# A decoder of two layers: values issued in pairs of steps, key and query stacks loaded in two parts, and the second layer's projections half by half

## The chip, the cores and the metric

The kernel runs on 1 core of a Trainium2 chip. The time is that of the device, in microseconds (us), from one launch to its end; of several runs the median is given. Engines: TensorE (PE), VectorE (DVE), ScalarE (ACT), GpSimd (POOL), and SyncE (SP), whose queue issues all the DMAs.

## The reference, cut to what matters

Four batch elements (B = 4) of T = 1024 rows with D = 256 columns, and for each a context of S = 154 rows. Every sublayer is a residual with a layer norm (eps 1e-5) ahead of it:

```python
# layer 0: causal attention of 16 heads of 16, keys and values gated by a memory of Pluecker lines
scores = einsum('bhtd,bhsd->bhts', q, k_enh) * SCALE; softmax over s <= t; @ v_enh; @ out_w + out_b
# layer 0: cross attention to the context, rotary q and k, causal mask over s <= t
# layer 0: feed forward, rows and weights quantised, depthwise convolution of 3, silu
# layer 1: full attention, 16 heads of 16
q, k, v = jnp.split(x @ w_in.T + b_in, 3, axis=-1)
w = softmax(einsum('bhqd,bhkd->bhqk', q, k) / sqrt(d)); out = einsum('bhqk,bhkd->bhqd', w, v) @ w_out.T + b_out
# layer 1: one wide head over the context; then 16 experts of 128, the best 2 of each row, and a shared one
```

## The kernel before, in words

`build_program` (from L233) writes one program for each engine, and each runs through the same trip four times, one for each batch element (`tensor_program` at L2106, `scalar_program`, `vector_program`, `gpsimd_program`, `sync_program` at L2185). Nothing orders the engines but semaphores: `up(name, key)` marks an instruction, `at(name, key)` is the value to wait for. A trip has these stages: gated projections, heads of the first layer ("own"), output projection, cross attention ("cross"), feed forward ("feed"), heads of the second layer ("second"), the wide head, the experts.

**Stacks.** Scores are matmuls in bf16 of parts. A query or key value in f32 is cut into high, middle and low parts of bf16: ACT writes the high part, DVE the rest, ACT the middle part, DVE or POOL the low one. A head's stack has 96 rows, six parts of 16 rows (STACK = 6), so that one product sums the six part products. Queries and keys of all heads lie in `q_cut` and `k_cut` as slots [6, 2, 1024] (L505 to L520): queries high, middle, low, high, middle, high; keys high three times, middle twice, low. The repeated slots are copied: `double_queries` at L1169 and `double_keys` at L1174, each a copy of 2048 columns and one of 1024, on DVE or POOL. Then SP moves each head of a pair of heads with one DMA of 192 KB, 16 partitions x 6 slots into 96 rows (`load_queries` L860, `load_keys` L866). There are 3 places for pairs of the own and second heads and 6 for queries of the cross heads; the cross keys of all 16 heads are moved before, in 16 DMAs of 28.9 KB (`context_sync`, L1351).

**Order of the heads.** `attention_plan` (L160) writes one list of pieces, and each engine goes through it and does its own. `main` is the list of scores and values, a value step being put behind as soon as the scores of later steps make two groups; between entries of `main` come the pieces of the first pass, spread evenly. The pieces, with their lines:
- first (L646): scores of a tile of 128 rows with 512 keys into one of three banks (4 to 6), used in turn by first, top, spin, turn, context and wide pieces alike (`ring`, L591); DVE takes the maximum of each row (L796), which frees the bank.
- top (L725): the 32 maxima of a pair of heads, cut in three parts on POOL (L846 to L849), are transposed on PE, copied on ACT (L769), and a DMA of 12 KB (L909) puts them as three more rows of the query stack.
- score (L674; L678 the mask): both heads of a pair, 128 keys and up to 512 rows each, with those rows, into two banks; there are two such pairs of banks. ACT takes the exp of both in one instruction (L756), into one of four places in `probs`.
- value (L708): values of one step of 128 keys times the probabilities, two heads and odd and even tiles as four tiles of 32 columns of the array, summed up in bank 7. After the last step ACT copies it (gather, L763), PE transposes it (spin, L717) and DVE divides by the sum (norm, L812, L814).
- fill (L1438, `busy_tensor`): matmuls whose result nobody reads.

`heads_sync` (L877) is SP's order: first loads for all places, one after the other, then, in the order of the plan, top rows and the loads of the pair that takes a freed place.

**Around the heads.** `cross_vector`, `cross_scalar`, `cross_gpsimd` (L1370 to L1415) rotate and cut the cross queries in four units (half 0 of both groups of heads, then half 1), then double each group. In `tensor_program` 26 fillers and 6 more stand ahead of the cross heads. `feed_tensor` (L1440) ends with 26 fillers and the four turns (transposes, L481, copied by ACT, L488), 12 fillers between turns 1 and 2. `second_tensor` (L1571) then projects the keys and queries of the second layer in eight units of 4 matmuls: keys of group 0, half 0 and 1, queries of group 0, half 0 and 1, then group 1, and 9 fillers. `second_vector` and `second_gpsimd` cut and double them.

## Time and profile before

| | |
|---|---|
| median of 3 runs | 3350.33 us (3348.94 to 3357.76) |
| the profiled execution | 3356.7 us, its span 3355.1 us |
| mean granted TensorE clock | 0.996 |
| busy: PE, PEld, DVE, ACT, POOL | 95%, 51%, 69%, 53%, 19% |
| bytes by DMA | 147.74 MB, 18.1% of 16 engines' span on the hardware queue |
| trip 2 | 866 to 1694 us: own heads from 930, cross heads from 1113, feed from 1187, second heads from 1282 to 1495, experts to 1694 |

A matmul's end is modelled, and matmuls overlap by about 0.17 us, so a busy PE does not say that it is used to its limit: the starts do. Idle time in brackets stands before an instruction, with what ended it. A record of the value step comes twice for each matmul, since f32 goes through in two passes.

### The profile page before, as it was taken

Reading aid. Unit: us, or ns where it says so; the run is one execution under the profiler, and the core shown is the slowest. Engines: PE = TensorE matmul, PEld = TensorE weight load, DVE = VectorE, ACT = ScalarE, POOL = GpSimd, SP = SyncE. Lnnn points to the kernel's source line nnn. Section 1 sums busy time; section 2 is a strip of 40 time slices with the busy share of each in tenths; the row PEclk is TensorE's granted clock in tenths of the full one; section 3 lists DMA queues with packets and bytes.
Section 4 is the critical chain, followed back from the end, with each engine's and each line's share of the span. In section 5 each row is a group of like instructions: output and inputs, shape, how many; then the busy total and the mean of one; then the engine's idle time right before and its main releaser. Section 6 shows DMA issues by size and latency. Waiting matters only on the chain.

```text
span 3355.1 us, 46975 instructions
## 1 busy us (share of the span) xinstructions
PE 3191.1 (95%) x17720; PEld 1713.3 (51%) x17720; DVE 2323.0 (69%) x4331; ACT 1782.8 (53%) x2551; POOL 634.7 (19%) x1166
## 2 busy tenths in 40 slices
PE   6999889999999989999999998999999999899999
PEld 4444433378644443337864444334786444433477
DVE  7856688556685578856678557885667855788555
ACT  3565546643456555664355555566424655556632
POOL 0322010024132201012403120100340321020033
PEclk9999999999999999999999999999999999999999
DMA  3212011023121202111312020120231202021023
GB/s 138 51 34 39 1 34 34 11 65 114 32 52 26 40 1 38 30 35 53 115 38 43 18 40 1 39 39 25 63 105 42 40 17 39 5 44 30 10 84 96
DMA packets 118101, 147.74 MB, mean 44 GB/s; under 512 B 25384, under 2 KB 75920, under 8 KB 117596
## 3 DMA queue, kind: packets, MB, share of 16 engines
q1 hardware_dynamic: 117876, 144.74, 18.1%
q8 instruction: 141, 2.31, 0.3%
q14 instruction: 84, 0.69, 0.1%
HBM read 74.25 MB, written 4.46 MB: 23 GB/s over the span
## 4 chain that ended last, share of the span: by engine, by line
PE 51%; DVE 8%; ACT 4%; issue 2%; DMA 1%; SPq 1%; POOL 0%; DVEq 0%; ACTq 0%
PE psum L1908 13%; PE psum L708 9%; PE psum L674 8%; PE psum L646 7%; PE psum L1000 4%; DVE small L796 3%; ACT work L756 2%; PE psum L939 1%; PE psum L717 1%; PE psum L500 1%; DMA work<-work 1%; PE psum L481 1%; PE psum L929 1%; SPq L863 1%; PE psum L1734 1%
## 5 line engine op out<-in xcount | busy, mean ns | idle before, releaser
L796 DVE TENSOR_REDUCE small<-psum 128x1 f32<-128x512 f32 (+6 forms) x1856 | 1136.7, 656 | 210.2 <-PE psum L646 175.9
L756 ACT ACTIVATE work<-psum 128x1024 f32<-128x1024 f32 (+5 forms) x1024 | 918.3, 935 | 419.4 <-PE psum L674 317.4
L646 PE MATMUL psum<-work 96*128 96x512 bf16 (+4 forms) x2688 | 655.7, 308 | 32.8 <-DVE small L796 16.2
L1908 PE MATMUL psum<-rounded_work 128*128 128x512 f32 x2592 | 602.0, 394 | 9.9 <-DVE rounded_work L1994 6.5
L674 PE MATMUL psum<-work 99*128 99x512 bf16 (+4 forms) x2048 | 564.2, 358 | 6.9 <-ACT work L756 4.0
L1908 PEld LDWEIGHTS psum<-rounded_work 128*128 128x128 f32 x2592 | 489.9, 190 | 116.0 <-DVE rounded_work L1994 8.3
L708 PE MATMUL psum<-work 128*32 128x512 f32 (+4 forms) x4480 | 532.3, 528 | 1.6 <-ACT work L756 1.4
L646 PEld LDWEIGHTS psum<-work 96*128 96x128 bf16 x2688 | 233.5, 97 | 544.4 <-DVE small L796 332.2
L674 PEld LDWEIGHTS psum<-work 99*128 99x128 bf16 (+1 forms) x2048 | 178.5, 97 | 199.3 <-ACT work L756 63.1
L2009 ACT CAST rounded_work<-work 128x512 fp32r<-128x512 f32 x144 | 89.4, 621 | 344.5 <-DVE work L2050 321.7
L846 POOL CAST small<-small 128x16 bf16<-128x16 f32 x96 | 18.8, 196 | 1156.2 <-DVE small L803 586.8
L1438 PE MATMUL psum<-ident_bf 128*128 128x512 bf16 x808 | 201.3, 380 | 8.7 <-DVE work L1539 4.5
L812 DVE RECIPROCAL small<-psum 128x16 f32<-128x16 f32 x96 | 24.7, 257 | 243.1 <-PE psum L717 243.1
L2055 DVE TENSOR_TENSOR rounded_work<-work,rounded_work 128x512 fp32r<-128x512 f32 x144 | 118.4, 822 | 107.2 <-ACT rounded_work L2009 107.2
L1885 POOL CAST rounded_work<-work 128x256 fp32r<-128x256 f32 x192 | 100.3, 523 | 435.9 <-PE psum L1908 421.8
L708 PEld LDWEIGHTS psum<-work 128*32 128x32 f32 (+1 forms) x4480 | 94.0, 107 | 171.4 <-issue 143.9
L2045 DVE TENSOR_TENSOR work<-work,psum 128x512 f32<-128x512 f32 x144 | 98.7, 685 | 99.5 <-PE psum L1908 89.4
L1886 POOL TENSOR_TENSOR rounded_work<-work,rounded_work 128x256 fp32r<-128x256 f32 x192 | 148.1, 772 | 15.4
L1438 PEld LDWEIGHTS psum<-ident_bf 128*128 128x128 bf16 x808 | 77.8, 98 | 93.1 <-DVE work L1539 7.8
L2050 DVE TENSOR_TENSOR work<-work 128x512 f32<-128x512 f32 x128 | 114.2, 892 | 14.7 <-DMA work<-combine 10.4
L1000 PE MATMUL psum<-xT,qkv 128*128 128x512 f32 x256 | 113.1, 593 | 2.7 <-ACT xT L488 2.7
L1000 PE MATMUL psum<-xT,work 128*128 128x512 f32 x256 | 110.5, 592 | 0.0
(297 smaller groups left out, 3765.2 us busy)
## 6 DMA issues: line engine op xcount, KB each, us to landing
work<-work SPq DMA_DIRECT2D x320, 192.0 KB, 4.3
work<-combine SPq DMA_DIRECT2D x64, 512.0 KB, 4.1
work<-in_w_gate SPq DMA_DIRECT2D x64, 128.0 KB, 3.5
work<-in_w_up SPq DMA_DIRECT2D x64, 128.0 KB, 3.5
work<-in_w_down SPq DMA_DIRECT2D x64, 128.0 KB, 3.8
work<-in_x SPq DMA_DIRECT2D x8, 512.0 KB, 4.9
out<-x SPq DMA_DIRECT2D x8, 512.0 KB, 2.9
work<-work SPq DMA_DIRECT2D x64, 28.9 KB, 2.0
```

Of the source, the lines that this page charges most:

```text
L646: ins = nc.tensor.matmul(dst[:, c * n:(c + 1) * n], A.q_pair[0:ROWS, slot, h, P * i:P * (i + 1)], A.k_of(pair, h)[0:ROWS, s0:s0 + n], star ...
L674: ins = nc.tensor.matmul(dst[0:size, 0:P * many].rearrange("p (i c) -> p i c", c=P), A.k_of(pair, h)[0:MORE_ROWS, P * s:P * s + size], til ...
L708: ins = nc.tensor.matmul(dst, V_head, moving, start=(s == 0), stop=(s == A.ns - 1), skip_group_check=True)
L756: nc.scalar.activation(probs[0:size, n % 4, :, 0:P * many], banks(2 * (n % 2), 2)[0:size, :, 0:P * many], ACT.Exp, scale=DH ** -0.5).then_ ...
L796: nc.vector.tensor_reduce(tops[:, pair % 2, places[0]:places[-1] + 1:step], src, AX.X, ALU.max) \
L1000: ins = nc.tensor.matmul(out, w[:, a, P * k:P * (k + 1)], xT[:, a, 1 + HALF * half:1 + HALF * (half + 1)], start=(a == 0), stop=(a == KD - 1))
L1438: nc.tensor.matmul(bank(place).rearrange("p (a c) -> p a c", c=P), ident_bf[:, :], spread(ident_bf[:, :], 1, 4), start=True, stop=True, sk ...
L1885: pool_own(nc.gpsimd.tensor_copy(shape(hi_w), source))
L1886: ins = nc.gpsimd.tensor_tensor(shape(lo_w), source, shape(hi_w.bitcast(F32)), ALU.subtract)
L1908: ins = nc.tensor.matmul(dst, a_parts[i], b_parts[j], start=start and n == 0, stop=stop and n == 2, skip_group_check=True)
L2050: nc.vector.tensor_tensor(value, value, row[e % 2][:, HALF * half:HALF * (half + 1)], ALU.mult).then_inc(*up("unit_full", u))
L2055: nc.vector.tensor_tensor(hid_low[:, u % 4, :], value, hid_high[:, u % 4, :].bitcast(F32), ALU.subtract).then_inc(*up("unit_ready", u))
```

## The change

What it does:
- `attention_plan` puts two value steps of a pair behind one another, and `probs` has 6 places instead of 4.
- The slots are put in another order (queries middle, middle again, low, high; keys low, middle, high, high again): four slots instead of six are used, only one part is copied (512 or 1024 columns, `high_again`, `middle_again`, on POOL, for cross queries on ACT), and `double_queries` and `double_keys` are gone. A head's stack is moved in two DMAs: high parts of the queries (one slot read three times) and middle and low ones; of the keys middle to high again, and low to high. The first pair's upper half is moved before its low parts are cut.
- Cross keys are no longer moved ahead for all heads but by pair, with the queries, in the same way.
- The order of the second layer's units is keys and queries of half 0, then of half 1; unit 0 is projected between turns 1 and 2 of the feed stage.
- 12 fillers there become 2, 9 behind the units 2, 26 ahead of the cross heads 14. The second heads no longer wait for unit 6 at their entry, but their banks for units 4 to 6.
- wide_q is not kept for the whole run but loaded into freed space in each trip, after the last stacks.

```diff
+PROBS = 6
@@ attention_plan
-    def value(pair, s):
-        pieces = [("value", pair, s)]
-        if s == len(steps) - 1:
+    def values(pair, s):
+        pieces = [("value", pair, s), ("value", pair, s + 1)]
+        if s + 1 == len(steps) - 1:
...
-            while sum(len(steps[later]) for _, later in held[1:]) >= 2:
-                value(*held.pop(0))
-    for which in held:
-        value(*which)
+            while sum(len(steps[later]) for _, later in held[2:]) >= 2:
+                values(*held[0])
+                held = held[2:]
+    for which in held[::2]:
+        values(*which)
@@ build_program
+        Q_MIDDLE, Q_MIDDLE_TOO, Q_LOW, Q_HIGH = range(4)
+        K_LOW, K_MIDDLE, K_HIGH, K_HIGH_TOO = range(4)
-        probs = area.take(4, 2, HALF)
+        probs = area.take(PROBS, 2, HALF)
@@ ring
-                by, n, had = {}, 0, [None] * 3
+                by, n, had = {}, 0, [("second_rest", 4 + j) if self.tag == "second" else None for j in range(3)]
@@ load_queries, load_keys
-                nc.sync.dma_start(A.q_pair[0:ROWS, slot, h, :], q_cut[r + DH * h:r + DH * (h + 1), :, k, :]) \
-                    .then_inc(*up(LOADED[2 * slot + h], A.tag, pair, by=16))
+                src, dst = q_cut[r + DH * h:r + DH * (h + 1), :, k, :], A.q_pair[:, slot, h, :]
+                if low is not True:
+                    nc.sync.dma_start(dst[0:UPPER, :], spread(src[:, Q_HIGH], 1, 3)).then_inc(*up(LOADED[2 * slot + h], A.tag, pair, by=16))
+                if low is not False:
+                    nc.sync.dma_start(dst[UPPER:ROWS, :], src[:, Q_MIDDLE:Q_LOW + 1]).then_inc(*up(LOADED[2 * slot + h], A.tag, pair, by=16))
...
+                if low is not True:
+                    nc.sync.dma_start(dst[UPPER:ROWS, :], src[:, K_MIDDLE:K_HIGH_TOO + 1]).then_inc(*up(LOADED[2 * slot + h], A.tag, pair, by=16))
+                if low is not False:
+                    nc.sync.dma_start(dst[0:UPPER, :], src[:, K_LOW:K_HIGH + 1]).then_inc(*up(LOADED[2 * slot + h], A.tag, pair, by=16))
@@ heads_sync, cross and second
+                for low in (False, True):
+                    keys_ready(0, low)
+                    load_keys(A, 0, low)
+                if a == "cross":
+                    for pair in (1, 2):
+                        load_keys(A, pair)
+                for low in (False, True):
+                    queries_ready(0, low)
+                    load_queries(A, 0, low)
+                for pair in range(1, A.slots):
+                    if pair == 4:
+                        keys_ready(1)
+                        queries_ready(1)
+                    if a == "second" or pair > 2:
+                        load_keys(A, pair)
+                    load_queries(A, pair)
@@ context_sync
-            for head in range(H):
-                k, r = head // 8, DH * (head % 8)
-                sp.wait_ge(*at("context_cut", k))
-                nc.sync.dma_start(ctx_stacks[0:ROWS, head, :], ctx_cut[r:r + DH, :, k, :]).then_inc(*up("context_keys_landed", by=16))
@@ cross_vector
-            cross_doubles(0)
             cross_rest(3)
-            cross_doubles(1)
@@ feed_tensor
                 if j == 1:
-                    busy_tensor(12)
+                    second_unit_tensor(0)
+                    busy_tensor(2)
@@ second_tensor
-        second_units = [(name, k, half) for k in range(KD) for name in ("k", "q") for half in range(2)]
+        second_units = [(name, k, half) for k in range(KD) for half in range(2) for name in ("k", "q")]
...
-            busy_tensor(9, 0)
+            busy_tensor(2, 0)
@@ second_vector
-            double_keys(nc.vector, k_cut, 0, "first_doubled", "k", 0)
...
-            double_queries(nc.vector, 0, "first_doubled", "q", 0)
@@ tensor_program
-            busy_tensor(26, cross_banks[0])
+            busy_tensor(14, cross_banks[0])
```

## Rows read from the trace of the kernel before

**Rows 1.** The page, busy time, share of the span and instructions:

```profile
PE 3191.1 (95%) x17720; PEld 1713.3 (51%) x17720; DVE 2323.0 (69%) x4331; ACT 1782.8 (53%) x2551; POOL 634.7 (19%) x1166
```

**Rows 2.** Timeline of PE, projections, then second heads: start us, us, engine, line:

```profile
1266.28 14.00 PE L1000 MATMUL psum<-xT,qkv 128*128 128x512 f32 x32 [0.68 <-ACT xT L488]
...
1319.55 0.38 PE L646 MATMUL psum<-work 96*128 96x512 bf16 x1
1319.86 1.07 PE L708 MATMUL psum<-work 128*32 128x512 f32 x8
1320.86 0.39 PE L646 MATMUL psum<-work 96*128 96x512 bf16 x1
1321.09 0.60 PE L674 MATMUL psum<-work 99*128 99x512 bf16 x2
...
1322.70 1.06 PE L708 MATMUL psum<-work 128*32 128x512 f32 x8
```

**Rows 3.** Timeline of ACT in the same cycle:

```profile
1321.72 1.94 ACT L756 ACTIVATE work<-psum 128x1024 f32<-128x1024 f32 x2 [0.90 <-PE psum L674]
```

**Rows 4.** Timeline, first pass ahead of the second heads' scores, PE and DVE:

```profile
1284.39 0.81 PE L646 MATMUL psum<-work 96*128 96x512 bf16 x3
...
1284.81 5.47 DVE L796 TENSOR_REDUCE small<-psum 128x1 f32<-128x512 f32 x9 [0.39 <-PE psum L646]
1285.56 0.39 PE L646 MATMUL psum<-work 96*128 96x512 bf16 x1 [0.36 <-DVE small L796]
```

**Rows 5.** Timeline of PE, end of the own heads, three value steps:

```profile
1074.88 1.08 PE L708 MATMUL psum<-work 128*32 128x128 f32 x20
```

**Rows 6.** Timeline, a top piece of the second heads, PE and SP:

```profile
1326.85 0.24 PE L725 MATMUL psum<-ident_bf,small 128*48 128x128 bf16 x1
...
1327.41 0.74 SPq L909 DMA_DIRECT2D work<-work  x1
```

**Rows 7.** DMA issues, KB each, median us from issue to landing:

```profile
work<-work SPq DMA_DIRECT2D x64, 28.9 KB, 2.0
```

**Rows 8.** Timeline of PE, start, tail and end of the second heads:

```profile
1282.28 0.38 PE L646 MATMUL psum<-work 96*128 96x512 bf16 x1
...
1488.50 1.07 PE L708 MATMUL psum<-work 128*32 128x512 f32 x8
...
1490.46 1.07 PE L708 MATMUL psum<-work 128*32 128x512 f32 x8
...
1495.09 0.70 PE L929 MATMUL psum<-x,ident 128*128 128x512 f32 x1
```

**Rows 9.** Timeline around the cross heads' start, SP, POOL and PE:

```profile
1060.50 11.15 SPq L1357 DMA_DIRECT2D work<-work  x16
...
1106.83 1.16 POOL L1414 TENSOR_TENSOR work<-work 128x512 bf16<-128x512 f32 x1 [3.69 <-ACT work L1382]
1109.63 13.27 SPq L863 DMA_DIRECT2D work<-work  x12
1113.31 0.24 PE L646 MATMUL psum<-work 96*128 96x154 bf16 x1 [0.49 <-DMA work<-work]
...
1122.94 2.11 SPq L909 DMA_DIRECT2D work<-work  x2
1126.07 0.60 PE L674 MATMUL psum<-work 99*128 99x512 bf16 x2
```

**Rows 10.** Timeline of PE, then stretches: us, busy by engine, PEclk, DMA share, GB/s:

```profile
1540.29 0.96 PE L1908 MATMUL psum<-rounded_work 128*128 128x512 f32 x3 [1.62 <-DVE rounded_work L1994]
1547.60:1551.00 3.40, 3.40 (x10) 2.65 (x9) 3.19 (x29) 2.09 (x3) 0.00 (x0) 0.50 0.01 2
```

**Rows 11.** Timeline of PE, start of the own heads:

```profile
930.72 0.40 PE L646 MATMUL psum<-work 96*128 96x128 bf16 x4 [0.41 <-DMA work<-work]
```

**Rows 12.** Timeline, fillers between the turns, PE, and a middle part, ACT:

```profile
1261.17 2.75 PE L1438 MATMUL psum<-ident_bf 128*128 128x512 bf16 x12
...
1272.32 0.61 ACT L1605 CAST work<-work 128x512 bf16<-128x512 f32 x1
```

More of the change, by code:

```diff
@@ L560, in build_program @@
         wide_v = area.take(2, D)
+        wide_q = area.take(KD, D)
         area.at = WIDE_AT
@@ L696, in heads_tensor @@
                                 i0, _, many = A.steps[s][part]
-                                moving = probs[0:size, A.number[(pair, s, part)] % 4, h, 0:P * many]
+                                moving = probs[0:size, A.number[(pair, s, part)] % PROBS, h, 0:P * many]
                                 dst = bank(7)[rows, P * (i0 // 2):P * (i0 // 2 + many)]
@@ L908, in heads_sync @@
                         sp.wait_ge(*at("scored", a, A.last_of(pair - A.slots, A.ns - 1)))
+                    if a == "second" and pair == PAIRS_OF_HEADS - 2:
+                        for loaded in range(PAIRS_OF_HEADS - SLOTS, PAIRS_OF_HEADS):
+                            for h in range(2):
+                                sp.wait_ge(*at(LOADED[2 * (loaded % SLOTS) + h], a, loaded))
+                        nc.sync.dma_start(wide_q, io["wide_q"]).then_inc(*up("wide_q_landed", by=16))
                     nc.sync.dma_start(A.q_pair[ROWS:MORE_ROWS, slot].rearrange("p h (i c) -> p (h i) c", c=P), top_rows[0:PARTS * TH, pair % 2, :]) \
@@ L1151, in keys_high @@
             act.wait_ge(*at("keys_full", n))
[L1152 removed]
+            nc.scalar.copy(half_of(k_cut[:, K_HIGH], k, half), raw_half(k_raw, k, half)).then_inc(*up("keys_high", n))
         def keys_middle(n):
@@ L1591, in second_scalar @@
         def second_scalar():
-            for n, (name, k, half) in enumerate(second_units):
-                _, bias, cut, _, parts = second_parts[name]
-                act.wait_ge(*at("second_projected", n))
-                nc.scalar.activation(half_of(cut[:, parts[0]], k, half), bank(n), ACT.Identity, bias=resident[bias][:, k:k + 1]).then_inc(*up("second_high", n))
+            for n in range(len(second_units)):
+                if n:
+                    second_high(n)
                 if n not in (0, 4):
@@ L1599, in second_scalar, with second_high @@
                     second_middle(n)
+        def second_high(n):
+            name, k, half = second_units[n]
+            _, bias, cut, _, parts = second_parts[name]
+            act.wait_ge(*at("second_projected", n))
+            nc.scalar.activation(half_of(cut[:, parts[0]], k, half), bank(n), ACT.Identity, bias=resident[bias][:, k:k + 1]).then_inc(*up("second_high", n))
         def second_middle(n):
@@ L1638, in second_gpsimd @@
             for n, (name, k, half) in enumerate(second_units):
-                if n < 4:
-                    continue
                 _, _, cut, rest, parts = second_parts[name]
-                pool.wait_ge(*at("first_doubled", "q", 0))
-                pool.wait_ge(*at("second_middle", n))
-                nc.gpsimd.tensor_tensor(half_of(cut[:, parts[2]], k, half), raw_half(rest, k, half), half_of(cut[:, parts[1]], k, half), ALU.subtract) \
-                    .then_inc(*up("second_cut", n))
@@ L1661, in second_banks_free @@
-        def second_banks_free(queue):
-            queue.wait_ge(*at("second_rest", 6))
+                if n >= 4:
+                    pool.wait_ge(*at("second_rest", "cut", 3))
+                    pool.wait_ge(*at("second_middle", n))
+                    nc.gpsimd.tensor_tensor(half_of(cut[:, parts[2]], k, half), raw_half(rest, k, half), half_of(cut[:, parts[1]], k, half), ALU.subtract) \
+                        .then_inc(*up("second_cut", n))
+                if name == "k":
+                    pool.wait_ge(*at("second_high", n))
+                    high_again(k_cut, 2 * k + half, "second")
+                else:
+                    pool.wait_ge(*at("second_middle", n))
+                    middle_again(2 * k + half, "second")
@@ new lines, in second_queries, with second_keys @@
+        def second_queries(k, low=True):
+            if low:
+                sp.wait_ge(*(at("second_cut", 7) if k else at("second_rest", "cut", 3)))
+                sp.wait_ge(*at("part_again", "second", "q", 2 * k + 1))
+            else:
+                sp.wait_ge(*at("second_high", 4 * k + 3))
+        def second_keys(k, low=True):
+            sp.wait_ge(*at("part_again", "second", "k", 2 * k + 1))
+            if low:
+                sp.wait_ge(*(at("second_cut", 6) if k else at("second_rest", "cut", 2)))
+            else:
+                sp.wait_ge(*at("second_middle", 4 * k + 2))
```

190 lines of the change are left out of this document (84 added, 106 removed).

## The prediction, before the changed kernel was run

> **What bounds the kernel now.** I read the busy line of the page first [rows 1]: TensorE (PE) is busy 95% of the span, so the question for each edit is whether PE gets shorter, or whether another engine or the SyncE queue (SP) makes it wait. The profiled execution took 3356.7 us (span 3355.1); the median shown is 3350.3. All four trips look alike, so I cost one trip (times of the second one, 866 to 1694 us) and multiply by four.
>
> I call a first-pass unit F, one matmul group of a score step S, a value step V. The timeline of the second layer's heads [rows 2] shows a cycle that repeats: F, V, F, S, F, F, S, F, V. An F costs PE 0.215 us, an S 0.435. V's first matmul starts 0.31 after the F before it, 0.095 more than that F needs, and the next F starts 1.00 later; its streams are two of 0.427 (the projections' matmuls, 512 columns in f32, take 0.43 each [rows 2]), so some 0.145 is overhead. The cycle is 4 x 0.215 + 2 x 0.435 + 1.095 = 2.83 us, and V follows V at 2.84 [rows 2]: PE waits for nothing here. ScalarE (ACT) starts an exp 0.41 after the second matmul of its S and needs 1.02, or 0.92 from start to start when the next is ready [rows 3]. VectorE (DVE) starts the maximum of an F 0.42 after it; nine in a row take 5.47 us, 0.598 apart and 0.68 long; and an F that waits for a bank starts 0.06 after that maximum ends [rows 4]. So DVE has work for 2.4 of 2.83 us, and ACT for 1.9.
>
> **The change, part by part, per trip.**
>
> 1. *Values in pairs.* The plan has 61 + 15 + 63 separate stretches of V in the three head stages, and 31 + 8 + 32 after: 68 joins. Where V already follows V, three steps joined (20 records, the same 0.85 us of streams as one V of 512 columns) take 1.08 us to their end [rows 5], and one alone 1.07 [rows 2]: two joins, and no more overhead than one V has. A join so saves about 0.095 + 0.1 = 0.19 us of PE, 68 x 0.19 = 12.9 us a trip if nothing else waits. The Trainium skill (TensorEngine Tiling (Array Packing), Key Properties) says that a change of tiling mode drains the engine; the trace agrees, and by that rule alone part 1 would bring the whole 12.9 us.
>
> But V makes no F. In the new order a regular cycle of the second layer is V V F F S F S F F S F F S F. I walk it with the durations above, 0 being F1, DVE idle by then: the maxima start at 0.42, 1.03, 1.63, 2.22, the fourth ends at 2.90. F7 reuses the bank of F4 (a ring of three), so it starts at 2.96, though PE has reached it at 2.62. Then S, F8, entry and two V: 0.215 + 0.435 + 0.215 + 0.095 + 1.90 = 2.86, cycle 5.82 against 2 x 2.835 = 5.67. PE alone would take 5.47. So a regular cycle gets 0.15 longer, not 0.19 shorter. In the cycle with the top rows, the transposition is now 2.1 us of PE work ahead of the S that needs the landed rows (3.3 before); from it to SP's issue pass 0.56 us [rows 6]; the landing takes 2.0 us for 28.9 KB [rows 7] and at most the 3.1 of the cross heads below; I take 2.25. So S waits 0.8, in which the banks come free: 5.47 + 0.17 + 0.8 = 6.43 against 2.84 + 3.12. The cycle with the spin: 6.59 against 6.49, walked in the same way. Pair: 2 x 0.13 + 0.48 + 0.10, +0.85 on 23.7. In the tail without F, V follows V at 1.97 [rows 8], 3.93 for two steps; joined, ACT has its two buffers full during V V and idles at its end. In the order V V, S5a, S5b, S6a, S6b, V V, S6a starts not before exp 5a ends (0.22 + 0.41 + 1.02 + 0.06 = 1.71 after V V), S6b not before exp 5b (0.92 later, 2.63), then 0.44, entry and V V, 1.99: 5.06. Walked so over all of the plan, the stage of before takes 214.0 us (shown: from 1282.3 to 1495.1 [rows 8], 212.8), after 222.6: **+8.5** (lead +1.1, six middle pairs +4.9, tail +2.4). The same walk gives the first layer's heads +0.5 (pair 15.9 to 15.8, tail +0.9) and the cross heads +1.4 (6.2 to 6.6 a pair). Bounds for the three: -12.9 (only PE counts) and +12.
>
> 2. *Stacks in two DMAs per head, and cross keys loaded by pair.* Work on DVE and GpSimd (POOL) shrinks (one part copied again instead of three), but SP issues more: a pair takes 8 DMAs, not 4, and cross pairs take key DMAs too. Before the cross heads SP issued 12 query DMAs in 13.27 us and only then the first top rows [rows 9]; the first S ran at 1126.07, 3.1 us after their issue at 1122.94 and right behind ten fillers [rows 9]. After: pair 0's high parts go out early; its low ones can at 1108.1, when POOL has cut the third unit [rows 9]; with 2.9 to land, between 2.0 [rows 7] and the 3.7 from 1109.63 to 1113.31 of a whole stack [rows 9], F starts at about 1111.0 instead of 1113.3: the lead is 2.3 us early. Then come 2 low DMAs, 8 for the queries of pairs 1 and 2, 24 for pairs 3 to 5: 34, with the top rows behind them. What does half a stack cost to issue? The trace has none. 192 KB and 28.9 KB both take 0.64 from issue to issue where the transfers don't hold SP up (16 in 11.15 us with one long one, [rows 9]), so bytes don't set it; below, 0.55 for the 22 query DMAs by bandwidth (13.27/12/2) and 0.3 for key ones; above, the top rows' DMA, 0.74 and 0.04 to the next [rows 6]. I take 0.64, the nearest row: 34 x 0.64 = 21.8, so top rows are issued at 1129.8, landed 2.25 later at 1132.1, and the first S runs then: **+6.0** (ends: 0 and +10.7). The Trainium skill (DMA: Bandwidth & Descriptors, Rules for kernel authors) says to join many small transfers into a large one, since under 64 KB one pays mostly overhead. The two sizes at one price agree; by bytes alone the 12 key halves would be nearly free and S0 no later than before.
> PE has run out of work by then at about 1124 (its ten fillers end at 1126.07 less the 2.3 of the early lead), so it idles some 8 us. A granted clock of 0.50, the lower of the two levels (1.2 GHz), is seen for 3.4 us, 7 us behind an idle time of 1.62 us [rows 10]; half speed for one such stretch costs **+1.7** (ends 0, +3.4). Later loads (8 DMAs, 5.1 us) and the rows behind them fit in their slack of 8.5 us.
> First layer: the second head of pair 0 waited for its DMA until 930.72 [rows 11]; without the doubling on DVE it lands by 929.9 and PE is ready then: **-0.6** (0 to -0.8).
>
> 3. *Second layer's projections.* Unit 0 (4 matmuls, 1.72 us) and 2 fillers, 0.43, take the place of 12 fillers, 2.75, between two turns [rows 12]: hidden, PE is ready for the turn in time; if the copy of the second turn were late, it would cost 1.72. The block behind it shrinks from 32 matmuls, 13.8 us [rows 2], to 28, 12.0, and ends at 1278.3. The keys' middle part of half 1 is ready as the third unit's is now, 1272.32 + 0.61 [rows 12], so SP issues from 1273.0, 8 DMAs at 0.64, the last for head 0 at 1276.8; the keys' cut takes DVE 0.7 from there, that of the queries comes one unit (1.7) later at 1275, both ahead of their DMAs; 2.9 to land, as above: F at 1279.7 instead of 1282.28 [rows 8]: **-2.6** (-3.6 to -1.2). Late next: DVE's last rest at 1280.0, hidden.
>
> 4. *The rest.* wide_q comes from HBM once a trip, issued most of a pair ahead of its use, 256 KB beside idle DMA engines: 0. Fewer fillers elsewhere: nothing, except for the clock in 2. The six slots of probabilities only make the joins possible: 0.
>
> Sum: 8.5 + 0.5 + 1.4 + 6.0 + 1.7 - 0.6 - 2.6 = +14.9 us a trip, x 4 = +60. On 3356.7 that is 3417; against the median, 3350.3 + 60 = **3410 us, 1.8% slower**.
>
> **Rivals.**
> *A. Only PE counts (faster).* Maxima and exps keep up, since DVE has 15% to spare, and the SP queue is cheap. Then -12.9 - 0.6 - 2.6 - 2.3 (early cross lead) = -18.4 a trip, at most -74: 3277; with half of the joins' worth, 3302. It decides in this way if PE gains more at a join than the bank ring makes it lose: under 0.15 us of wait a cycle. Against it: the walk, which meets the order of before within 1.5 us of 213.
> *B. Pairing costs, the SP queue doesn't.* Half DMAs issue at 0.3 to 0.5: cross +1.4 - 1.5 (the early lead kept in part), no clock loss: +8.5 + 0.5 - 0.1 - 3.2 = +5.7, x 4: 3373.
> *C. The SP queue costs, pairing pays half.* 6.0 + 1.7 - 6.5 (half of 12.9) - 3.2 = -2, x 4: 3342, and 3358 with a little less of the joins, no change that can be told.
> *D. The change doesn't do what it says*: unit 0 finds no gap (turn 2 late by 1.7) and the low parts land no sooner, so that part 3 is 0: forecast + 4 x 2.6, 3420. It stays inside the forecast's range.
>
> **Chances.** Both mechanisms as in the sum 0.50 (own range 3380 to 3440), B 0.20, C 0.12, A 0.18. 0.3% (10 us) is about what a measurement of this kernel can tell from no change. Faster: A and a part of C, 0.21; same: most of C and the edge of B, 0.10; slower 0.69. The range takes in B and C and the upper ends (pairing +12, issue 0.78: 25 a trip would be 3450, seldom all at once): 3325 to 3440.
>
> **What would show it.** Right: in the second layer's heads PE waits of about 0.3 us before L646's matmul, ended by DVE's maximum, once or twice a cycle of 5.8 us; S after top rows waiting for a DMA; the stage 222 us long; the first cross S at 1132 minus what came before, with a DMA wait of 8 us and a granted clock of 0.5 behind it; F of the second layer 2.6 us earlier after the turns. Wrong: V V cycles of 5.5 us with DVE never idle over 0.3, or half DMAs on SP under 0.4 apart.

## The result, and the profile after

The changed kernel takes 3442.47 us (median of 4 runs, 3440.49 to 3447.13), the kernel before 3353.89 beside it: a ratio of 1.0267, 95% interval 1.0247 to 1.0287. It is 88.6 us slower. The forecast was 60 slower, the range ended at 3440. The direction was right, the size too small, and the time lies above the range, by 2 us.

The page's busy line of the kernel after answers to [rows 1]:

```profile
PE 3180.1 (92%) x17604; PEld 1730.9 (50%) x17604; DVE 2270.0 (66%) x4283; ACT 1792.1 (52%) x2567; POOL 632.4 (18%) x1182
```

PE, DVE and POOL are busy for a little less than before, ACT for 9 us more (1792.1 against 1782.8), in a span 86 us longer: most of the time went into waits. PE's busy time hides a part, though, since work at half clock counts as busy for longer. The mean granted clock fell from 0.996 to 0.982. Where the time went shows from three starts that PE's timeline has in each head stage: the first F (a unit of the first pass, L650 now), the first S (the matmuls of a score step, L678), the last V (a value step, L712). Means over the four trips, us:

| stretch | before | after | difference |
|---|---|---|---|
| own heads, first F to last V | 144.7 | 143.7 | -1.0 |
| from there to the first cross F | 37.7 | 35.0 | -2.7 |
| cross, first F to first S | 12.7 | 22.7 | +10.0 |
| cross, first S to last V | 48.6 | 59.7 | +11.1 |
| from there to the first F of the second heads | 107.7 | 105.05 | -2.6 |
| second heads, first F to last V | 212.4 | 220.8 | +8.4 |
| from there to the next own F (three times) | 264.9 | 263.0 | -1.8 |

Four times the first six and three times the last are +87.3; the two profiled spans differ by 86.4. The loss stands in two places: the cross heads, +21.1 a trip, and the second heads, +8.4; the other stretches gained.

SP's timeline of the kernel after, cross heads of trip 2 (start, us it was busy, count), answers to [rows 9]. L870 and L872 are query halves, L881 and L883 key halves, L936 the top rows:

```profile
1126.66 1.21 SPq L872 DMA_DIRECT2D work<-work  x2
1127.91 0.59 SPq L870 DMA_DIRECT2D work<-work  x1
...
1135.24 0.59 SPq L883 DMA_DIRECT2D work<-work  x1
1135.87 0.59 SPq L870 DMA_DIRECT2D work<-work  x1
...
1148.62 0.59 SPq L872 DMA_DIRECT2D work<-work  x1
1149.25 1.58 SPq L936 DMA_DIRECT2D work<-work  x2
```

Key halves (14.4 KB) and query halves (96 KB) are both 0.63 to 0.64 apart, but for three that took longer. 34 loads from 1126.66 to 1149.25 are 22.6 us, where the forecast had 21.8. PE's timeline beside it:

```profile
1129.35 0.24 PE L650 MATMUL psum<-work 96*128 96x154 bf16 x1 [0.47 <-DMA work<-work]
...
1134.89 0.24 PE L729 MATMUL psum<-ident_bf,small 128*48 128x128 bf16 x1 [0.45 <-POOL small L853]
...
1138.65 2.33 PE L1450 MATMUL psum<-ident_bf 128*128 128x512 bf16 x10
1152.16 1.01 PE L678 MATMUL psum<-work 99*128 99x512 bf16 x2 [11.17 <-DMA work<-work]
...
1161.20 3.79 PE L712 MATMUL psum<-work 128*32 128x512 f32 x16
...
1187.83 2.06 PE L712 MATMUL psum<-work 128*32 128x512 f32 x16
```

The maxima of pair 0 were transposed on PE at 1134.89, 14.4 us before SP came to its rows. PE ran dry at 1140.98 and idled 11.17 us. Then comes what the forecast did not have in this size: S takes 1.01 us where it takes 0.60, and two value steps take 3.79 at 1161 but 2.06 at 1188. The stretches view says why (PE busy, then the granted clock, DMA share, GB/s):

```profile
1131.00:1144.30 13.30, 8.75 (x68) 1.00 0.61 97
1144.31:1175.03 30.72, 22.87 (x106) 0.50 0.35 54
1175.03:1215.00 39.97, 37.55 (x278) 1.00 0.01 3
```

For 30.72 us the granted clock is 0.50, 1.2 GHz. It falls 3.3 us after PE ran dry, and it stays there for 22.9 us of work behind the first S. All four trips have this stretch, with the same length.

PE's timeline of the second heads answers to [rows 2]:

```profile
1346.73 0.39 PE L650 MATMUL psum<-work 96*128 96x512 bf16 x1 [0.15 <-DVE small L800]
...
1347.70 1.92 PE L712 MATMUL psum<-work 128*32 128x512 f32 x16
...
1353.50 1.92 PE L712 MATMUL psum<-work 128*32 128x512 f32 x16
...
1359.37 1.93 PE L712 MATMUL psum<-work 128*32 128x512 f32 x16
...
1364.46 0.61 PE L678 MATMUL psum<-work 99*128 99x512 bf16 x2 [0.80 <-DMA work<-work]
...
1366.08 1.92 PE L712 MATMUL psum<-work 128*32 128x512 f32 x16
```

The regular cycle, V V to V V, takes 5.80 and 5.87; the walk had 5.82. S behind the top rows waits 0.80, as the walk had it, and this cycle takes 6.71 (walk: 6.43). Four starts of V V make one pair of heads, and the starts say where a pair loses. Before, the same four take 5.67, 5.67, 5.99 (with the top) and 6.40 (with the spin), now 5.80, 5.87, 6.65 to 6.73 and 6.42. So some 0.7 of the 1.0 us that a pair loses stands in the cycle with the top rows, 0.3 in the two regular ones.

The waits view, from 1342 to 1520 us (us in total, times, the longest):

```profile
PEld psum L650 <- DVE small L800: 43.5, 91, 0.8
...
PE psum L678 <- DMA work<-work: 5.5, 6, 1.6
PEld psum L678 <- ACT work L760: 5.2, 16, 0.8
...
PE psum L650 <- DVE small L800: 1.3, 8, 0.2
```

And the same view of the kernel before, from 1308 to 1480 us:

```profile
PEld psum L646 <- DVE small L796: 46.2, 60, 0.8
```

A lesson in reading: the wait for maxima stands at the weight load of F (PEld), 91 times and 43.5 us; at PE's matmul it is 1.3 us in all. Neither number is the loss. Before, where V follows V at 2.84 and PE loses nothing in a regular cycle, the weight loads wait for maxima 46.2 us too, since a load waits beside the matmuls ahead of it, which still run. The starts of V tell what the idle columns don't.

PE's timeline ahead of the second heads, with unit 0 between the turns (L484), answers to [rows 12]:

```profile
1299.25 1.98 PE L1025 MATMUL psum<-xT,qkv 128*128 128x512 f32 x4 [0.68 <-ACT xT L491]
1301.07 0.59 PE L1450 MATMUL psum<-ident_bf 128*128 128x512 bf16 x2
1301.54 1.30 PE L484 MATMUL psum<-ident,xn 128*128 128x128 f32 x8
1303.52 12.28 PE L1025 MATMUL psum<-xT,qkv 128*128 128x512 f32 x28 [0.68 <-ACT xT L491]
1315.64 0.59 PE L1450 MATMUL psum<-ident_bf 128*128 128x512 bf16 x2
1316.95 0.39 PE L650 MATMUL psum<-work 96*128 96x512 bf16 x1 [0.72 <-DMA work<-work]
```

Unit 0 fits in the gap, and the first F is 2.6 us earlier behind the last cross V, the forecast's number.

### The profile page after: what moved, and what is told of

It is laid out like the page before. It is cut to its first block and busy times, and to the rows that moved or that the text cites. A ratio compares the mean times of both kernels' runs of the same rounds, so it can differ in the third digit from the quotient of the medians.

```text
span 3441.5 us, 47034 instructions
## 1 busy us (share of the span) xinstructions
PE 3180.1 (92%) x17604; PEld 1730.9 (50%) x17604; DVE 2270.0 (66%) x4283; ACT 1792.1 (52%) x2567; POOL 632.4 (18%) x1182
## 5 line engine op out<-in xcount | busy, mean ns | idle before, releaser
L800 DVE TENSOR_REDUCE small<-psum 128x1 f32<-128x512 f32 (+6 forms) x1856 | 1106.8, 654 | 346.0 <-PE psum L650 331.2
L650 PE MATMUL psum<-work 96*128 96x512 bf16 (+4 forms) x2688 | 655.9, 312 | 38.6 <-DVE small L800 21.8
L678 PE MATMUL psum<-work 99*128 99x512 bf16 (+4 forms) x2048 | 581.4, 367 | 87.8 <-DMA work<-work 64.7
L1931 PE MATMUL psum<-rounded_work 128*128 128x512 f32 x2592 | 594.4, 390 | 9.9 <-DVE rounded_work L2017 6.5
L712 PE MATMUL psum<-work 128*32 128x512 f32 (+4 forms) x4480 | 489.4, 533 | 2.5 <-ACT work L760 2.4
L650 PEld LDWEIGHTS psum<-work 96*128 96x128 bf16 x2688 | 234.8, 99 | 494.5 <-DVE small L800 299.0
L678 PEld LDWEIGHTS psum<-work 99*128 99x128 bf16 (+1 forms) x2048 | 174.9, 98 | 277.1 <-ACT work L760 86.8
L712 PEld LDWEIGHTS psum<-work 128*32 128x32 f32 (+1 forms) x4480 | 118.3, 109 | 222.7 <-issue 195.5
L1450 PE MATMUL psum<-ident_bf 128*128 128x512 bf16 x692 | 175.5, 379 | 8.7 <-DVE work L1553 4.5
L841 POOL TENSOR_SCALAR_AFFINE_SELECT work<-work 128x256 f32<-128x256 f32 x160 | 64.1, 406 | 239.5 <-ACT work L760 237.1
## 6 DMA issues: line engine op xcount, KB each, us to landing
work<-work SPq DMA_DIRECT2D x128, 14.4 KB, 1.9
```

Source lines behind the costliest of these rows:

```text
L650: ins = nc.tensor.matmul(dst[:, c * n:(c + 1) * n], A.q_pair[0:ROWS, slot, h, P * i:P * (i + 1)], A.k_of(pair, h)[0:ROWS, s0:s0 + n], star ...
L678: ins = nc.tensor.matmul(dst[0:size, 0:P * many].rearrange("p (i c) -> p i c", c=P), A.k_of(pair, h)[0:MORE_ROWS, P * s:P * s + size], til ...
L712: ins = nc.tensor.matmul(dst, V_head, moving, start=(s == 0), stop=(s == A.ns - 1), skip_group_check=True)
L800: nc.vector.tensor_reduce(tops[:, pair % 2, places[0]:places[-1] + 1:step], src, AX.X, ALU.max) \
L1450: nc.tensor.matmul(bank(place).rearrange("p (a c) -> p a c", c=P), ident_bf[:, :], spread(ident_bf[:, :], 1, 4), start=True, stop=True, sk ...
L1931: ins = nc.tensor.matmul(dst, a_parts[i], b_parts[j], start=start and n == 0, stop=stop and n == 2, skip_group_check=True)
```

## The experiments

Two theories at the start. The first: the SP queue makes the first cross S late, PE's idle time brings the clock down, and pairing costs the second heads 8.4. The rival: pairing makes the cross heads longer too, through the bank ring. The edits are against the kernel after, the times are medians, and the kernel before took 3350.19, 3351.36, 3352.88 and 3354.72 us (one run) in the four groups of runs.

**More fillers while PE would idle.**

```diff
-[(n, ("fill", 1 if n < 15 else 10)) for n in range(16)]
+[(n, ("fill", 1 if n < 15 else 60)) for n in range(16)]
```

> 60 fillers instead of 10 stand ahead of the first S of the cross heads; 50 more at 0.213 us are 10.7 us, about the idle time of 11.2 there. The queue is as it was, so the first S is as late as before. Theory (the half-speed stretch follows from the idle time and is worth half of the 23 us of PE work in it): the granted clock stays at 1.0 and the cross heads behind the first S take 48 to 50 us instead of 59.6: -10 to -11.4 a trip, 3398 us. Rival (the cross heads are longer through pairing and the bank ring): no change, 3442 us. Rival 2 (the clock falls anyway, with the DMA load): 3442 us, the low stretch still there.

3422.44 us (ratio to before 1.0206, 1.0185 to 1.0227), 20 faster than after. First S 22.7 behind F, unchanged. The stretches view of trip 2 (busy times of PE, PEld, DVE, ACT and POOL, then the clock):

```profile
1126.00:1149.00 23.00, 21.28 (x134) 10.85 (x135) 8.71 (x18) 2.50 (x5) 2.75 (x9) 1.00 0.62 94
1149.00:1165.00 16.00, 15.03 (x121) 6.97 (x120) 8.42 (x18) 11.25 (x15) 6.20 (x9) 1.00 0.38 57
```

The clock stays at 1.0 in the cross heads of three trips (the fourth has 3.41 us at 0.50), and the stretch behind the first S falls from 59.7 to 51.9 (mean of four), 50.9 in trip 2. The edit does nothing there but fill PE's idle time, so it is the idle time that brings the clock down, and that costs 7.8 to 8.8 us a trip. The second rival, the DMA load, has fallen: from 1126 to 1149 us the DMA share is 0.62 in both kernels. The size expected, 10 to 11.4, was half of the 22.9 us at low clock. A pair of cross heads takes 11.56 at half clock and 7.01 at full, so part of it was waits that don't stretch: 22.9 x (1 - 7.01/11.56) = 9.0. And only 20 of some 31 us came out in the end: six short stretches at 0.50 (3.41 and 6.83 us, 24 us together), which after does not have, came up, three behind the second heads, and one each in the own, the cross and the second heads. The kernel before has such stretches too. Why after has none was not tested.

**Half as many.** The same line with 34.

> 34 fillers instead of 10: the idle time ahead of the first S falls from 11.2 to some 6.0 us and nothing else changes. If the clock falls after any idle time of several us, the half-speed stretch is still there and the time is 3442 us; if it falls only after the longer one, the granted clock stays 1.0 and the time is 3398 us; a shorter low stretch (3.4 or 6.8 us, as the trace of before has them) gives some 3405 to 3410.

3438.14 us (one run). Two of four trips have 23.89 us at 0.50 and a cross stage as long as after's (82.3 and 82.6), two have 13.65 us and stages of 77.1 and 77.8. None of the three expectations holds for all trips: the clock still falls, and the time that it stays low doesn't follow from the idle time (5.75 and 5.36 us in trips 1 and 2, with 23.89 low; 5.11 and 5.85 in trips 3 and 4, with 13.65).

**Value steps one by one.** `attention_plan` as before, PROBS stays 6:

```diff
-        pieces = [("value", pair, s), ("value", pair, s + 1)]
+        pieces = [("value", pair, s)]
...
-                values(*held[0])
-                held = held[2:]
+                value(*held.pop(0))
```

> The value steps are issued one by one again, in the order of before; the six places of probabilities and all else stay. Theory (the join is paid back by the bank ring and by top rows that come later): second heads 220.8 to 212.3 (-8.5), own heads +0.6, cross heads -1.4 to -3.5 (7.0 to 6.5 a pair once the clock is back): -9.3 to -11.4 a trip, about 3401 us. Rival (only PE counts, a join saves 0.19 us): the 68 stretches more cost +12.9 a trip, 3494 us.

3387.76 us (1.0106, 1.0087 to 1.0125), 55 faster than after. Second heads 212.3, as before to the tenth; own heads 144.0 (+0.3). The first cross S is as late as in after (22.8), but the stretch behind it is 52.3, not 59.7. The rival (+52) has fallen. The stretch behind the first S lost 7.4, of which pairing is 2.3 (by keys_ahead_rows_first, below); the other 5.1, more than expected, is clock. The stretches view of this kernel, trip 2, its first S at 1139.92:

```profile
1128.10:1131.90 3.80, 0.10 (x1) 1.00 0.48 65
1131.91:1148.98 17.07, 9.06 (x42) 0.50 0.40 62
1148.98:1180.00 31.02, 30.77 (x252) 1.00 0.13 21
```

PE idled 11.72 us here, a little more than in after, and yet only 9.1 us of work ran at half clock, against 22.9. The one difference in PE's work behind the first S is the order of V. How the two hang together was not settled. So the idle time costs 8.8 a trip by the clock with pairs of V, but only 3.7 with single ones (52.3 against before's 48.6).

**Top rows ahead of the last stacks.** The stacks of pairs 4 and 5 move behind the top rows of pairs 1 and 2:

```diff
-                for pair in range(1, A.slots):
+                for pair in range(1, min(A.slots, 4)):
...
+                    if a == "cross" and pair in (1, 2):
+                        load_keys(A, pair + 3)
+                        load_queries(A, pair + 3)
```

> In the cross heads SP issues the stacks of pairs 4 and 5 only behind the top rows of pairs 1 and 2, so 18 of the 34 loads still stand ahead of the first top rows, not 34. Theory (the SP queue makes the first S late, and the idle time makes the clock fall): the top rows of pair 0 are issued some 10.7 us earlier, PE idles under 1.5 us ahead of the first S, the stretch of 30.7 us at a granted clock of 0.5 is gone, which gives back another 11 us: -21.7 a trip, 3355 us. Rival 1 (the clock falls for another reason): only -10.7 a trip, 3400 us, the low stretch still there. Rival 2 (pairing in the cross heads is what costs, PE would wait for banks instead): under -5 a trip, over 3420 us.

3411.62 us (1.0178, 1.0158 to 1.0198), 31 faster, not 87. The first S did come in time (12.1 behind F, less than before's 12.7). But SP issues 8 loads for a pair, 5.1 us, and pair 4's, pair 5's and those for the freed place queue up. SP's and PE's timelines:

```profile
1141.99 0.78 SPq L933 DMA_DIRECT2D work<-work  x1
1142.81 0.59 SPq L881 DMA_DIRECT2D work<-work  x1
...
1153.75 16.12 SPq L933 DMA_DIRECT2D work<-work  x3
```

```profile
1156.02 1.04 PE L678 MATMUL psum<-work 99*128 99x512 bf16 x2 [4.32 <-DMA work<-work]
```

16 loads stand between two top rows, S of pair 3 waits 4.32 us, and the clock falls there: 1.04 for this S. My edit had moved the queue, not shortened it.

**Cross keys ahead again**, in halves, in `context_sync`, where SP has time:

```diff
+            for head in range(H):
+                src, dst = ctx_cut[r:r + DH, :, k, :], ctx_stacks[:, head]
+                nc.sync.dma_start(dst[UPPER:ROWS, :], src[:, K_MIDDLE:K_HIGH_TOO + 1])
+                nc.sync.dma_start(dst[0:UPPER, :], src[:, K_LOW:K_HIGH + 1])
...
         def load_keys(A, pair, low=None):
+            if A.tag == "cross":
+                return
```

> The cross keys are loaded ahead again, in halves (32 DMAs once the context keys are cut, in the own heads), and leave the queue of the cross heads: 22 loads instead of 34 ahead of the first top rows. Theory (each load ahead of the rows costs 0.64 us, whatever it carries): 12 fewer, top rows 7.6 us earlier, the first S at 15 us behind F instead of 22.8, idle time under 4 us; the cross stage then is 82.4 - 7.6 and, where the granted clock stays at 1.0, 8.3 less again (what busy_through gave), of which some 3 us a trip come back in short low stretches elsewhere as there: 3390 us, or 3412 if the clock still falls. Rival (the loads are bound by bytes; keys are small): first S less than 3 us earlier, over 3425 us.

3402.05 us (1.0155, 1.0135 to 1.0176). First S at 14.8 behind F (expected 15): 12 loads fewer, of 14.4 KB each, are 7.9 us, 0.66 a load. So a small load costs as much as a large half. The clock falls in the cross heads in all trips still, but for 3.4 to 17 us, and the stretch behind the first S is 53.8 in the mean.

**Both together.**

> As keys_ahead, and the queries of pairs 4 and 5 only behind the top rows of pairs 1 and 2. In rows_first the same order left SP behind by pair 3 (8 loads a pair are 5.1 us, and three pairs of loads stood between two top rows), and S of pair 3 waited 4.3 us. With 4 loads a pair SP keeps up. Theory: no wait for top rows over 1 us in the cross heads, granted clock 1.0 there, cross stage 63 to 65 us instead of 82.4; second heads still 220.8: -18 + 3 a trip, 3380 us. Rival (what rows_first left is due to pairing in the cross heads and not to SP): the stage stays over 70 us, over 3400.

3370.14 us (1.0056, 1.0039 to 1.0073), 72 faster than after. SP and PE at the first S of trip 2:

```profile
1117.28 0.59 SPq L874 DMA_DIRECT2D work<-work  x1
1117.92 4.28 SPq L937 DMA_DIRECT2D work<-work  x2
```

```profile
1121.06 2.33 PE L1463 MATMUL psum<-ident_bf 128*128 128x512 bf16 x10
1123.22 0.60 PE L680 MATMUL psum<-work 99*128 99x512 bf16 x2
```

PE has no idle time ahead of S, which takes 0.60. The cross stage is 62.4 in every trip, 11.5 and 50.9. The clock is at 1.0 in all of them. This version says what the change costs without the queue: 50.9 - 48.6 = +2.3 for pairing in the cross heads (7.01 a pair against 6.49), and the second heads' 8.4. Which wait makes the 0.52 a pair in the cross heads was not taken apart.

**The rest of the change alone.** As the last, with single value steps:

> As keys_ahead_rows_first with the value steps one by one: what is left of the change is half stacks for queries and keys, no doublings, units half by half with unit 0 in the gap, wide_q by DMA. Theory: cross stage 61 us as before, second heads 212.3 as before, and the lead-ins stay as they are after (-2.7 ahead of the cross heads, -2.6 ahead of the second, -1.2 to -1.5 ahead of the own): -6.5 a trip against before, 3325 us, faster than both. Rival (the leads are short only because the stages behind them start at a worse point): about 3350.

3328.19 us (0.9933, 0.9916 to 0.9949): 23 us faster than before, little but clear of the noise, and 114 faster than after. Cross heads 60.1, second heads 212.4, the leads as after. So what parts 2 and 3 gain stays when the queue and the pairing are out of the way: 2.7 + 2.6 a trip at the leads, 1.2 at the first cross S, and the shorter way to the own heads.

**Pairs in the own heads only**, on top of that:

> As keys_ahead_rows_first, with pairs of value steps in the own heads alone and single steps in the cross and second heads. Theory: own heads 143.7 as in after, against 144.0 with single steps; cross 60.1 and second 212.3 as with single steps: 3328 - 1 = 3327 us, the same as keys_ahead_single.

3324.41 us (0.9914, 0.9896 to 0.9932), the lowest median, though the times can hardly tell it from the one above (3320.18 to 3327.95 against 3327.1 to 3332.47). The trace shows the own heads at 143.7 in all trips against 144.0.

**Unit 0 behind the turns.**

```diff
-                    second_unit_tensor(0)
-                    busy_tensor(2)
+                    busy_tensor(12)
...
-            for n in range(1, len(second_units)):
+            for n in range(len(second_units)):
```

> Unit 0 is projected behind the turns with the others, and the gap has its 12 fillers again; the order half by half and the waits on the ring stay. Theory: one unit, 1.72 us, comes back on PE ahead of the second heads: lead 105.0 to 106.7, +7 us in all, 3449 us; the other 0.9 us of the 2.6 gained come from the order of the units and the fillers. Rival (the lead is set by the DMAs of the first stack, not by PE): no change, 3442.

3453.37 us (1.0306, 1.0288 to 1.0323), 11 slower than after. The lead goes from 105.05 to 107.8. F itself waits some 0.7 us for the DMA of its stack in both kernels, but the DMAs start as PE's projections let them: the first key half is issued 6.7 us behind the start of the block of 28 matmuls in after (1303.52 to 1310.24) and here (1312.34 to 1319.07). So the rival has fallen, and the chain starts on PE. It is 2.8, not 1.72, since more than the unit comes back; PE's timeline:

```profile
1308.72 1.88 PE L1025 MATMUL psum<-xT,qkv 128*128 128x512 f32 x4
1312.34 12.29 PE L1025 MATMUL psum<-xT,qkv 128*128 128x512 f32 x28 [1.74 <-ACT xT L491]
```

ACT's program still has unit 0 ahead of the copies of turns 2 and 3, and held them until it was projected: 1.74 of wait instead of 0.68. That 1.06 belongs to my edit.

**Tops one F earlier** (TOP_LAG 3 for 4).

> The transposition of a pair's maxima stands one F earlier in the order (TOP_LAG 3 instead of 4), all else is as after. Theory (S behind the top rows waits 0.8 us for them once a pair, since the join has taken V out of the stretch between them): the top moves some 0.2 to 0.7 us ahead, the wait falls by as much unless GpSimd has not cut the maxima by then: second heads -1 to -4 us, cross heads, where PE waits 0.5 for GpSimd ahead of the top, no better: 3442 - 4 to 16 = 3426 to 3438 us. Rival (GpSimd's cut sets it): no change or slower, and the wait stands ahead of the top instead.

3499.01 us (1.0425, 1.0399 to 1.0452), 57 slower. PE reached the top before GpSimd had cut the maxima. From 1373 to 1560 us the weight load of the top waits for GpSimd (L853) six times, 11.0 us in all, a wait that the second heads of after don't have; own heads take 149.8, second 229. The rival was right; the order of after is the better one.

**What eats the joins.** Halved maxima, in both kernels; then exps of the second heads halved as well. These kernels leave out half of the columns that the maxima, or the exps, should read, and don't compute the right result:

```diff
-nc.vector.tensor_reduce(tops[...], src, AX.X, ALU.max)
+nc.vector.tensor_reduce(tops[...], src[:, :, 0:n // 2], AX.X, ALU.max)
...
+                    wide = P * many if a != "second" or n < PROBS else P * many // 2
-                    nc.scalar.activation(probs[0:size, n % PROBS, :, 0:P * many], ...
+                    nc.scalar.activation(probs[0:size, n % PROBS, :, 0:wide], ...
```

> The maxima of the first pass read half of the columns of each bank (256 of 512), so the kernel no longer subtracts the true maxima; all other work stays. VectorE then needs some 0.35 us per F, not 0.60. Theory (the bank ring eats the joins): the regular cycle V V to V V of the second heads falls from 5.80 to 5.87 to 5.47 us, four times 0.215 for the F in each half and so on with nothing waited for; what stays is the wait for top rows of 0.8 once a pair: top to top 24.75 to some 23.7, second heads 220.8 to about 213. Rival (a join costs PE something of its own, or ScalarE is what binds): cycle still over 5.7, stage over 219.

> The same cut of the maxima in the kernel before. Theory: PE waited for nothing in the regular cycle of before, so V to V stays 2.83 to 2.84 us, top to top 23.7 and the second heads 212 within 1 us. Against half_maxima_after the cycle then gives the price of a join with nothing in its way: 2 x 2.835 - 5.47 = 0.19 us. Rival (the ring was binding in before too): second heads under 210.

> Half of the columns in the maxima of all heads and, in the second heads, half in the exps (512 of 1024), so both the maxima and the probabilities are not the true ones; all other work stays. half_maxima_after brought the regular cycle only to 5.68, with ScalarE in four exps of 0.92 in a row and 1.91 idle while V V ran. Theory (then the two pairs of banks for scores bind: the second S pair waits for its exp): with exps of some 0.5 us nothing is waited for and the cycle is PE's own, 5.47 us, less at most by 0.02. Rival (a join is worth nothing to PE: the entry and exit cost belong to each step): 5.67, as it is now.

> The same two cuts in the kernel before. Theory: V to V stays at 2.83 to 2.84 us, since PE waited for neither engine in a regular cycle; second heads 207 us as with the maxima alone. Rival (exps were binding as well): V to V under 2.8.

> Only the exps of the second heads are cut in half, the maxima are whole. Theory (the ring of three banks is the longer of the two waits, the walk of the prediction): the cycle stays at 5.80 to 5.87 us, or falls by at most 0.1. Rival (the exps are the first cause and the waits for maxima follow from them): 5.5 to 5.6.

From V to V (two V in before's order), in the second heads of trip 2:

| | before, twice V to V | after, V V to V V |
|---|---|---|
| whole | 5.67 | 5.80 to 5.87 |
| exps halved | not run | 5.79 to 5.87 |
| maxima halved | 5.67 | 5.68 |
| both halved | 5.67 | 5.43 |

One run each: 3438.72 with the exps alone, 3377.82 and 3329.09 (after, before) with the maxima, 3362.76 and 3313.36 with both. With halved maxima I expected 5.47, and it stopped at 5.68. PE's timeline, then ACT's, with halved maxima:

```profile
1328.51 1.92 PE L712 MATMUL psum<-work 128*32 128x512 f32 x16
```

```profile
1325.76 3.77 ACT L760 ACTIVATE work<-psum 128x1024 f32<-128x1024 f32 x4 [1.91 <-PE psum L678]
1331.44 3.77 ACT L760 ACTIVATE work<-psum 128x1024 f32<-128x1024 f32 x4 [1.91 <-PE psum L678]
```

ACT idles 1.91 us while V V runs, since only two S fit in the banks, and then has four exps in a row, 3.77: 5.68 together. That is a second limit of its own. With both taken away (PE's timeline of half_both_after) the join pays:

```profile
1322.36 1.92 PE L712 MATMUL psum<-work 128*32 128x512 f32 x16
...
1327.79 1.93 PE L712 MATMUL psum<-work 128*32 128x512 f32 x16
```

5.43, and 2 x 2.835 - 5.43 = 0.24 us a join. Before's order stays at 2.84 through all three: PE waited for nothing there. The exps alone bring nothing in the regular cycle, because the ring is the longer of the two limits. So pairing takes 0.24 from PE's own work and meets a wall of 5.68 (scores' banks and exps) and one of 5.84 (ring and maxima).

The whole stage says more than the regular cycle (us from the first F to the last V, trips without a low stretch in it):

| | before | after |
|---|---|---|
| whole | 212.4 | 220.8 |
| maxima halved | 207.6 | 211.5 (one trip) |
| both halved | 205.6 | 204.2 |
| exps halved | not run | 217.1 |

- Halved maxima shorten before's stage by 4.8 us, though I expected 212 and had put under 210 as the sign that its ring binds. The regular cycle didn't move; 4.5 of it came out ahead of the first S (25.8 to 21.3 from the first F), where F after F waits for DVE [rows 4].
- Halved exps shorten after's stage by 3.7 us, at its end, where no F stands between the scores: two of the last V V cycles fall from 5.03 to 4.18. That is the tail of the walk.
- With both halved the joined order is only 1.4 us shorter than the single one, not 31 x 0.24 = 7.4: the cycle with the top rows still takes 6.65, and S still waits 0.75 for them. That wait is a third limit, and none of these cuts touches it.

## Why the prediction was right in direction and short in size

By the steps of its sum, us a trip:

| term | forecast | measured | from |
|---|---|---|---|
| second heads | +8.5 | +8.4 | stage, 212.4 to 220.8 |
| own heads | +0.5 | -1.0 | stage; -0.3 against single steps, some 0.4 low clock in one trip of before |
| cross heads, pairing | +1.4 | +2.3 | keys_ahead_rows_first, 50.9 against 48.6 |
| first cross S | +6.0 | +7.3 | -2.7 at the lead, +10.0 from F to S |
| clock | +1.7 | +8.8 | 59.7 against 50.9 |
| own lead | -0.6 | -1.4 | -1.8 in three of four, low clock in before with it |
| second lead | -2.6 | -2.6 | 107.7 to 105.05 |
| sum | +14.9 | +21.8 | x 4: 60 and 87 |

**The step that failed is the clock**, the term of +1.7 (ends 0 and +3.4), which measured +8.8. All of the seven missing us a trip are in it; the other errors (+1.3, +0.9, -0.8, -1.5) cancel, and that is luck. The mechanism was there, PE dry for 8 us and a stretch at 0.50 behind it, but its size was taken from [rows 10], 3.4 us behind an idle time of 1.62. The runs showed 22.9 us of work at 0.50 behind an idle time of 11.2. That the idle time would be five times as long as in [rows 10] stood in the prediction and was not used: the bound above was 3.4 us of loss, one such stretch twice over. The trace of before had no idle time of that length (none over 1.7 us behind its first 30 us, with stretches at 0.50 of 3.41 and 6.83), so nothing in it closed the range from above. The honest upper end, an estimate, was all of the work behind the first S at half speed, 48.6 us more a trip; I should have said so and let the range go well past 3440.

**The first cross S** came by its mechanism: price of a load 0.64 as taken, 34 of them in 22.6 us (21.8). From F to S in trip 2 it is 1.7 us longer than forecast (22.8, forecast 1111.0 to 1132.1): 0.8 by the queue, 0.7 by the landing (2.9 us from the issue of the rows at 1149.25 to S at 1152.16, where 2.25 was taken), 0.2 by the start of the loads. F came 0.4 earlier than forecast, which leaves 1.3.

**Pairing in the second heads** was right to a tenth in its sum and in the regular cycle (5.82 against 5.80 and 5.87), and partly by luck. A pair in the middle lost 1.0, not 0.85, mostly in the cycle with the top rows (6.65 to 6.73 against 6.43). Split at the tops of trip 2, the stage lost 0.0 up to the second top, 7.1 in the six pairs behind it and 1.7 from there to the end; the walk had 1.1, 4.9 and 2.4, as near as the two splits can be compared. The ring of three banks is the limit that binds in the regular cycle, as the walk had it. But the sentence that PE alone would take 5.47 hid a second limit at 5.68, which the walk did not need because the first lies above it: a faster maximum alone would not have brought 5.47.

**Pairing in the cross heads**, +2.3 for +1.4, was short: 0.52 a pair where the walk had 0.4, and its pair of 6.2 was 6.49 before.

**Rivals.** A (only PE counts) and C (pairing pays half) fell with steps_single, B (cheap issues) with SP's row: 0.64 a load. D was inside the forecast and did not come: unit 0 found its gap.

## What to carry to other kernels

A step that is batched on one engine starves those that feed on what is left out meanwhile: walk one cycle with the buffers between the engines, and do it once for each buffer, since taking away the first limit may show a second just behind it. Count a queue's entries, and not only its bytes, ahead of the one small transfer that everyone waits for, and put that one first only if the queue then keeps up to the end. And where a forecast makes TensorE idle for longer than any idle time in the trace, price the work behind it at half speed up to the whole stage, not by the short stretches that the trace has.

## What the runs showed of the hardware

The granted clock went to 0.50 for one stretch of 30.72 us in every trip of the kernel after (10.8 to 11.2 us idle, then work at full load), for 13.65 to 23.89 with 5.1 to 5.9 us idle (busy_half), for 17.07 with 10.9 to 11.7 us idle and another order of V behind it (steps_single), for 13.65 to 20.48 with 4.3 to 4.5 us idle (rows_first), for 3.41 to 17.07 with 2.9 to 3.5 us idle (keys_ahead), for 3.41 in one of four trips with fillers all through (busy_through), and not at all in the cross heads where S came in time (keys_ahead_rows_first). Within one kernel the longer idle time did not always bring the longer stretch. At half clock S takes 1.01 for 0.60, a joined pair of value steps 3.79 for 2.06. Kernels without the long stretch had short ones of 3.41 and 6.83 us elsewhere, the kernel after none (but for the one at its end), so filling the idle time gave back 20 us of 31.

A DMA inside the on-chip memory cost SP 0.64 us from one to the next, for 14.4 KB as for 28.9 and 96 KB. Stacks of 192 KB could be as close (0.64 between two of them in before's second heads), but the 12 ahead of before's cross heads took 13.27 us [rows 9], 1.1 each.

The profile's columns of idle time don't say what a wait costs: weight loads waited 46.2 us for maxima in a stretch of before where the regular cycle lost nothing, and 43.5 us in a like stretch of after, where it lost 0.12 to 0.20 a cycle.
